# Sums over tokens by four 32-row strips of TensorE instead of two 64-row strips

## What is computed

```
grouped      = x.reshape(B, S // 16, 16, 512)
logits       = einsum('bgtd,des->bgtes', grouped, controller) + tie      # 16 experts, 4 sets
perm         = (logits == max over the 16 tokens)
inner        = relu(einsum('bgtesf,bgtes->bgesf', grouped @ f1, perm))
result       = einsum('bgesd,bgtes->bgtd', inner @ f2, perm)
```

## Time and profile before

| what | value |
|---|---|
| median of 3 runs | 1988.45 us (1987.42 to 1990.15) |
| profiled execution, its own time | 1996.32 us |
| its span in the trace | 1994.6 us |
| mean granted TensorE clock | 0.973 of full speed |
| PE busy | 1851.7 us (93%) |
| DVE, ACT, POOL busy | 1189.4, 986.9, 363.8 us |

### The profile page before, as it was taken

One profiled execution on the slowest core, in us unless ns is written; L12 is line 12 of the kernel. 1 busy time (PEld: TensorE's weight loads), 2 busy tenths in 40 slices (PEclk: granted clock), 3 DMA queues, 4 the chain that ended last, 5 costly groups with the idle time before them and its releaser, 6 DMA issues. The chain is left out here.

```text
span 1994.6 us, 41286 instructions
## 1 busy us (share of the span) xinstructions
PE 1851.7 (93%) x15896; PEld 1361.5 (68%) x15896; DVE 1189.4 (60%) x2345; ACT 986.9 (49%) x1716; POOL 363.8 (18%) x428
## 2 busy tenths in 40 slices
PE   5486799999999999999999968999999999999999
PEld 3354678888888878888888766666666566666654
DVE  6488466666666543333333266776767767667655
ACT  2355223333333275665665345665656656556553
POOL 4486220000000000000000042222222222222210
PEclk9778899999999999999999999999999999999999
DMA  9987755666665373433443164444444435344322
GB/s 368 300 158 102 184 145 173 186 180 181 178 171 164 113 280 126 166 140 123 143 165 123 68 202 132 148 126 129 142 131 123 153 109 151 122 131 140 107 66 80
DMA packets 162434, 305.68 MB, mean 153 GB/s; under 512 B 15505, under 2 KB 87185, under 8 KB 159090
## 3 DMA queue, kind: packets, MB, share of 16 engines
q1 hardware_dynamic: 153327, 282.66, 44.8%
q0 software_dynamic: 8960, 20.98, 5.5%
HBM read 168.72 MB, written 134.87 MB: 152 GB/s over the span
## 5 line engine op out<-in xcount | busy, mean ns | idle before, releaser
L1542 PE MATMUL bank<-f2s,inner_bd 128*32 128x512 f32 x2528 | 295.5, 596 | 1.1 <-issue 1.0
L1425 ACT ACTIVATE inter_hi<-bank 128x512 fp32r<-128x512 f32 x316 | 188.3, 600 | 206.3 <-PE bank L1542 205.0
L598 ACT ACTIVATE h1o<-bank,b_by_channel 128x500 f32<-128x500 f32 x160 | 108.5, 678 | 324.8 <-PE bank L430 316.3
L1347 DVE TENSOR_TENSOR inter_lo<-bank,inter_hi 128x512 fp32r<-128x512 f32 x316 | 215.8, 689 | 88.2 <-ACT inter_hi L1425 87.2
L428 PE MATMUL bank<-hhi,w_hi 128*128 128x500 f32 x624 | 244.7, 392 | 0.0
L430 PE MATMUL bank<-hhi,w_lo 128*128 128x500 f32 x624 | 243.6, 390 | 0.0
L429 PE MATMUL bank<-hlo,w_hi 128*128 128x500 f32 x624 | 242.6, 389 | 0.0
L428 PE MATMUL bank<-ahi,w_hi 128*128 128x500 f32 x608 | 237.3, 390 | 0.0
L429 PE MATMUL bank<-alo,w_hi 128*128 128x500 f32 x608 | 236.6, 389 | 0.0
L430 PE MATMUL bank<-ahi,w_lo 128*128 128x500 f32 x608 | 236.4, 389 | 0.0
L562 DVE BATCH_NORM_STATS2 stats<-h1o 128x500 f32 (+1 forms) x160 | 103.3, 676 | 155.7 <-ACT h1o L598 155.7
(11 more groups left out here) (149 smaller groups left out, 3354.4 us busy)
## 6 DMA issues: line engine op xcount, KB each, us to landing
h1T<-h1o SPq DMA_DIRECT2D x19, 2000.0 KB, 8.1
h1in<-h1T SPq DMA_DIRECT2D x19, 2000.0 KB, 9.7
aggregate<-at SPq DMA_DIRECT2D x20, 1024.0 KB
x<-in_x SPq DMA_DIRECT2D x79, 256.0 KB, 2.7
x<-x SPq DMA_DIRECT2D x79, 256.0 KB, 3.4
x_back<-x SPq DMA_DIRECT2D x79, 256.0 KB, 3.1
out<-x_back SPq DMA_DIRECT2D x79, 256.0 KB, 2.1
h2in<-h2T SPq DMA_DIRECT2D x39, 512.0 KB, 4.1
```

Of the source, the lines that this page charges most:

```text
L598: nc.scalar.activation(h1o[b][:, m, :], mb[m % 4][:, 0:CW], ACT.Identity, bias=b1c[:, m:m + 1]).then_inc(evr, 1)
L1347: nc.vector.tensor_tensor(ilo[b][:, :], bI[b][:, :], ihi[b][:, :].bitcast(F32), ALU.subtract).then_inc(ilr, 1)
L1425: nc.scalar.activation(ihi[b][:, :], bI[b][:, :], ACT.Copy).then_inc(ihr, 1)
L1542: last = nc.tensor.matmul(bI[b][32 * i:32 * i + 32, :], ibd[:, e, j, :, :].rearrange("p s g -> p (s g)"), f2s[:, e, :], start=True, stop=True)
```

## The change

The rows of a tile are taken in four quarters of 32 instead of two halves of 64. Each quarter holds two groups, so `perm_bd` has 2 columns for each pair instead of 4, and each product has 128 columns. There are 32 products for a tile instead of 16. Each quarter has a PSUM bank of its own that takes all four chunks, so no bank is complete before the last products, and a copy moves the 512 elements of one quarter with runs of 2 elements (before: 4) in `yT`. All waits of the sums now stand ahead of its first product. The first quarter goes to bD[1], so `final` waits for one copy instead of two.

```diff
-GH = GB // 2
-HP = P // 2
+QR = 4
+GH = GB // QR
+HP = P // QR
...
-        bY, bF = [bD, bI[0:2]], bD[1]
+        bY, bF = [bD[1], bD[0], bI[0], bI[1]], bD[1]
...
-                            t, c = k * TB + n, KH - 2
-                            dve.wait_ge(yp, (t + 1) * KH)
-                            nc.vector.tensor_copy(yT[:, c:c + 2, :, n * GB + GH:(n + 1) * GB],
+                            t, r = k * TB + n, QR - 1
+                            dve.wait_ge(yp, (t + 1) * QR)
+                            nc.vector.tensor_copy(yT[:, :, :, n * GB + r * GH:n * GB + (r + 1) * GH],
...
-                def to_yT(k, j, c, r):
+                def to_yT(k, j, r):
                     t = k * TB + j
-                    act.wait_ge(yp, t * KH + c + r + 1)
-                    nc.scalar.activation(yT[:, c:c + 2, :, j * GB + r * GH:j * GB + (r + 1) * GH],
+                    act.wait_ge(yp, t * QR + r + 1)
+                    nc.scalar.activation(yT[:, :, :, j * GB + r * GH:j * GB + (r + 1) * GH],
...
-                    for h in range(2):
-                        if h and kb is not None:
-                            pe.wait_ge(ilr, lows(kb, j - 1 if crossing(kb, j) else j, 1))
-                        done = {}
-                        for c in (2 * h, 2 * h + 1):
-                            for part in (xhi, xlo):
-                                for r in range(2):
+                    if kb is not None:
+                        pe.wait_ge(ilr, lows(kb, j - 1 if crossing(kb, j) else j, 1))
+                    done = {}
+                    for c in range(KH):
+                        for part in (xhi, xlo):
+                            for r in range(QR):
...
-                    pe.wait_ge(yr, min((k * TB + j) * KH + 2, NT * KH) if k is not None else NT * KH)
+                    pe.wait_ge(yr, min((k * TB + j) * KH + 1, NT * KH) if k is not None else NT * KH)
```

More of the change, by code:

```diff
@@ L1362, in body @@
                         if what == "sums" and kb is None:
-                            t, c = k * TB + n, KH - 2
-                            dve.wait_ge(yp, (t + 1) * KH)
-                            nc.vector.tensor_copy(yT[:, c:c + 2, :, n * GB + GH:(n + 1) * GB],
-                                                  bY[c // 2][1][:, :].rearrange("p (c e g) -> p c e g", c=2, g=GH)).then_inc(yr, 1)
+                            t, r = k * TB + n, QR - 1
+                            dve.wait_ge(yp, (t + 1) * QR)
+                            nc.vector.tensor_copy(yT[:, :, :, n * GB + r * GH:n * GB + (r + 1) * GH],
+                                                  bY[r][:, :].rearrange("p (c e g) -> p c e g", c=KH, g=GH)).then_inc(yr, 1)
                         if what == "norm":
@@ L1401, in nonlinear @@
                                              scale=sc[:, c:c + 1]).then_inc(gr, 1)
-                def to_yT(k, j, c, r):
+                def to_yT(k, j, r):
                     t = k * TB + j
-                    act.wait_ge(yp, t * KH + c + r + 1)
-                    nc.scalar.activation(yT[:, c:c + 2, :, j * GB + r * GH:j * GB + (r + 1) * GH],
-                                         bY[c // 2][r][:, :].rearrange("p (c e g) -> p c e g", c=2, g=GH), ACT.Copy).then_inc(yr, 1)
+                    act.wait_ge(yp, t * QR + r + 1)
+                    nc.scalar.activation(yT[:, :, :, j * GB + r * GH:j * GB + (r + 1) * GH],
+                                         bY[r][:, :].rearrange("p (c e g) -> p c e g", c=KH, g=GH), ACT.Copy).then_inc(yr, 1)
                 def body(k, kb):
@@ L1415, in body @@
                                 act.wait_ge(inp, k * QB)
-                            for c in range(0, KH, 2):
-                                for r in range(2):
-                                    if kb is not None or c + r < KH - 1:
-                                        to_yT(k, n, c, r)
+                            for r in range(QR if kb is not None else QR - 1):
+                                to_yT(k, n, r)
                         if what == "unit":
@@ L1496, in sums @@
                         pe.wait_ge(otr, kb * TB + j)
-                    for h in range(2):
-                        if h and kb is not None:
-                            pe.wait_ge(ilr, lows(kb, j - 1 if crossing(kb, j) else j, 1))
-                        done = {}
-                        for c in (2 * h, 2 * h + 1):
-                            for part in (xhi, xlo):
[L1503 to L1510, removed]
+                    if kb is not None:
[4 more added lines that the diff above has]
+                            for r in range(QR):
+                                rows = slice(r * HP, (r + 1) * HP)
+                                done[r] = nc.tensor.matmul(
+                                    bY[r][:, c * ES * GH:(c + 1) * ES * GH],
+                                    part[j % 2][rows, c * P:(c + 1) * P],
+                                    pbd[rows, j % 2, :, :].rearrange("p e g -> p (e g)"), start=part is xhi, stop=part is xlo)
+                    for r in range(QR):
+                        done[r].then_inc(yp, 1)
                 def rows(k, kb, j):
```

## The result

The changed kernel is slower: 1996.9 us (median of 6 runs, 1994.46 to 2000.24) against 1989.39 us (6 runs of before). The ratio is 1.0036, with a 95% interval of 1.0025 to 1.0046. The forecast was no change at 1988.4 us, with a chance of 0.32 for slower. The time lies within the range given, on the side that was not forecast.

The account below looks back on a forecast made before the run. TensorE, busy 93% of the span, was taken to bound the kernel. Gains of 2.2, 1.3 and 1.6 us less losses of 3.9 and 1.2 made 0.0: no change, 1988.4 us by the median, range 1981.5 to 1999.

Parts of the forecast that it names:

- what bounds: Whole kernel: TensorE, busy 93% of the span, sets the end, so time taken from each tile's sums comes off.
- the new length of the sums: Each tile's sums: loads pace steps of 0.115 us, so 1.07 us instead of 1.15, 0.08 us less.
- Stream only: Rival, sums of every tile: 32-row loads hide or shrink, step 0.056 us, 32 us faster, 1956; chance 0.07.
- the strips add up: Rival, seven steps of every tile's sums: third and fourth strips lengthen the step to 0.134 us, 1998; chance 0.18.
- the copies and the waits: Around the sums: first copy 0.38 us later; waits of 0.12 us for `ilr` and 0.22 for `otr`.
- Tile 0's `final`: Tile 0: `final` held by the first copy, 1.98 us after the sums' start instead of 2.15; 1.5 us gained over 9.
- short runs: ACT's copies into `yT`: 8-byte runs taken as free, with up to 0.1 us each as the other bound.
- behind the first block: Later tiles: gains of 2.2 us in odd tiles, 1.3 in even tiles, 1.6 in tile 0 and the last tile.
- The crossings: Eight crossing tiles: copies start 0.38 us later, sums 0.11 later, delaying the third unit; 0.49 us lost each, 3.9 us.
- First block: 1.2 us lost.: First block: copies delay the silu TensorE waits for by 0.38 us in 4 pairs of tiles, less the odd tiles' gain.
- the odd tile gives 0.08 back.: First block: in each of 4 pairs, the odd tile's shorter sums return 0.08 us of the 0.38 us delay.
- copies get longer: Rival, at crossings, `final` and first block: short runs add 0.1 us to each copy, 8 us, 1996; chance 0.06.

Follow-up runs that it names:

- the second: The changed kernel run again with no edit: 1996.52 us, ratio 1.0035 to the kernel before.
- Late copies: Kernel before, two strips kept, but in the first block ACT's copies of the sums wait for the tile's last product: 1994.82 us, ratio 1.0031.
- filler alone: Changed kernel with 8 more products, results unread, ahead of the silu wait in each even tile of the first block: 1987.17 us, ratio 0.9992.
- the filler: Kernel before with 8 more products, results unread, ahead of the silu wait in each even first-block tile: 1987.26 us, ratio 0.9981.
- short stream: Changed kernel with the products of `xn_lo` streaming 64 columns instead of 128, loads as they were: 1996.65 us (one run).
- changed, all: Changed kernel, first-block silu ahead of copies, 8 unread products behind odd tiles' logits, DVE sharing crossing-tile copies, later `ilr` wait: 1981.72 us, ratio 0.9958.

## Why the prediction was wrong

The terms one by one; first two groups of lines of the changed kernel, the load by single line (ns min/median/max) and the copies from the page (us, mean ns):

```profile
L1503 PEld LDWEIGHTS bank<-perm_bd,xn_hi x1264: 181/187/329, 1166.6 to 1928.3; 32*128 32x128 f32 x181
```

```profile
L1407 ACT ACTIVATE yT<-bank 128x512 f32<-128x512 f32 x308 | 165.5, 629 | 57.4 <-PE bank L1503 57.4
```

- **Right: what bounds, and the new length of the sums.** The step of 0.115 measured 0.112, the sums' 1.07 us measured 1.07, and the loads are what paces them. The rule of the Trainium skill (TensorE: Matmul & The Clock Gate, section on LDWEIGHTS) that a load goes by its columns held: 187 ns by the median with 32 rows, 184 with 64. "Stream only" and "the strips add up" both fell. The "up to 4x" of the first stands in the Trainium skill's page TensorEngine Tiling (Array Packing) under Theoretical Speedup, not in the section that the prediction names; here four strips made the step 5% shorter.
- **Right: the copies and the waits.** First copy 1.14 us after the first load (1.16 said). `otr` in a crossing tile 0.22 us (0.22). In the even tiles the load unit idles 0.89 us ahead of the sums instead of 0.84: 0.05 lost, as said. Tile 0's `final` 2.03 us after the sums' start (1.98).
- **Set at nothing, and small: short runs.** The copies average 629 ns instead of 603, within the bound of 0.1 us given.
- **Right in kind, smaller in size: behind the first block.** The 62 gaps between sums that are no border took 506.5 us instead of 510.1, added up from the starts of the sums in the timelines: 3.6 us gained, where the terms for them made 5.1. The crossings give it back: 0.35 us of idle each and a start 0.10 later, 3.6 us for eight (3.9 said).
- **Wrong: "First block: 1.2 us lost."** This is the step that failed. The mechanism up to the wait was right: the silu wait grew to 2.10 us, where "about 2 us" was said. The sum priced it at the 0.38 us by which the chain moves, as if the clock stayed full. But half clock followed, in which the steps of the sums take 0.21 us instead of 0.11, for 3 to 7 us behind three of the four waits in the first profile and all four in the second. The first block took 5.9 us more in the first profile and 8.6 in the second.
- **Also wrong there: "the odd tile gives 0.08 back."** At full clock the two terms look like this: in the one pair of tiles of the changed kernel that ran at full clock throughout, the gap behind the even tile grew from 5.55 to 5.92 us, as said, but the one behind the odd tile shrank from 5.78 to 5.21. So the pair took 11.1 us instead of 11.3. The reason is DVE's mask `perm_new`, which took 0.76 us before and 0.29 now. Before, it ran beside GpSimd's `xn_lo`:

```profile
1200.88 1.26 POOL L1231 TENSOR_TENSOR xn_lo<-xn,xn_hi 128x512 fp32r<-128x512 f32 x1
...
1201.53 0.76 DVE L1320 TENSOR_TENSOR perm_new<-stats,logits_max 128x128 fp32r<-128x128 f32 x1
```

The mask ended 0.15 us after GpSimd's instruction. In the changed kernel GpSimd's had ended before (1200.00 + 1.27 = 1201.27, mask at 1201.39). At full clock the term would have been a small gain.

- No case and no rival of the forecast had the clock in it. The signs stood in the rows: a wait of 1.6 us in every even tile, in the part of the mixture where TensorE is least busy (37.79 of 50 us, the window shown above). Late copies alone made the kernel 5.9 us slower, filler alone made the changed one 9.4 us faster, and the clock's loss over all timed runs moved with both. That the longer wait costs time through the clock is shown by this.
- The time of 1996.9 us lies next to those of two rivals, "copies get longer" (1996) and "the strips add up" (1998). That is chance: the copies grew by 26 ns, not by 100, and the step is 0.112 us, not 0.134.
- Left open: the 4 us that the filler gains in the kernel before without the clock, and why the borders differ between executions (eight of them make 188.0 us in the one profile of before, 179.9 with the filler and 183.4 with the late copies, with the same code there). With such scatter a single profile can't prove where 7.5 us lie; the medians and the clock of all runs carry the argument.

## What to carry to other kernels

Where TensorE is the bound, a delay is not worth its own length if it falls into an idle of TensorE: look at each wait that it lengthens, ask whether the granted clock survives it, and price the following microseconds at half speed if it may not. Compare the mean clock of all timed runs, not only that of the profile. Look for such waits where the pipeline fills, not only where it runs. When strips are split further, the weight load stays; count it before counting columns.

## What the runs showed of the hardware

- Silu waits of 1.6 us in the kernel before were not followed by half clock (four of four). Waits of 2.1 us in the same place were, in three of four, four of four, two of four (late copies) and four of four (short stream), for some 3 to 7 us each (0.50 over 3.2 us and over 6.3 us in the windows shown). The length of one wait does not decide it alone: three of the sixteen long ones passed at full clock, and in "changed, all" the clock fell (0.50 from 1206.3 to 1209.5 us) though no wait of TensorE in the first block was longer than 1.21 us.
- Four strips of 32 rows load their weights at once: 0.112 us a step for four loads of 128 columns (with streams of 128 columns), against 0.118 for two (with streams of 256).
- ACT's copies into runs of 8 bytes took 26 ns more (4%) than those into runs of 16 bytes; no run changes the runs alone.
- In the 12 profiles, between 1160 and 1225 us, DVE's `perm_new` started 18 times while GpSimd's `xn_lo` was running. Each time it ended 0.14 to 0.16 us after GpSimd's, and took up to 1.39 us. At all other times but two (0.38 and 0.58) it took 0.29 us.
- The first load of a crossing tile's sums came 0.12 us after DVE's result when the wait for it was the last one in line, and 0.22 us when another wait stood behind it.
